# Moving one stage's weight preparation and statistics into the stage before it

## The chip, the cores and the metric

The kernel runs on one core of a Trainium2 chip. The metric is the device time of one execution in microseconds (us). Three timed runs of the kernel before gave 1868.03, 1863.23 and 1867.54 us; their median is 1867.54 us.

## The reference

Two decoder layers on x of 32 x 64 tokens of width 256 (2048 tokens in all). Every sub-layer normalises its input and adds its result to x. In order: layer 0 has a causal self-attention (16 heads of 128), a cross-attention to a context (16 heads of 8, no weights of its own), and a feed-forward block; layer 1 has a recurrent mixer, a cross-attention, and a feed-forward block with 4-bit weights. What matters here is the feed-forward block of layer 0:

```
n  = attention of 16 heads of 16 on rmsnorm(x, ln1_w)        # Wq, Wk, Wv, Wo
m  = modulation from n, through A (256 x 16) and B (16 x 1024)
h  = silu(z @ W_in.T + m @ B) * (z @ W_up.T)                 # z = rmsnorm(.., ln2_w), 1024 wide
x  = x + h @ W_down.T
```

W_in, W_up and W_down are 256 x 1024 matrices (1 MB each). The norm's weight ln2_w is folded into W_in and W_up by scaling their rows.

## The kernel before

All 2048 tokens stay in SBUF as 16 tiles of 128 rows (`core.x`). The kernel is five stages, one after the other; inside a stage each engine has its own instruction list, written by hand, and engines meet only through semaphores. A stage consists of blocks. At the end of a block all engines meet in a barrier. Between two stages there is one more such meeting, in which SyncE clears the semaphores (`run_stage`). `run_steps` orders an engine's list: at step s it issues, for each part with lag l, the work of unit s - l, parts in the order in which they are listed. So an instruction that waits holds up everything listed behind it on its engine.

**Full-precision products from two parts.** Matmuls of the feed-forward part take operands split into a high part (rounded to fp32r, a ScalarE copy) and a low part (the difference, a subtraction), and add three products.

**Stage 2, `stage_L0_cross`.** First `token_stats` turns the statistics of each row (`bn_stats`, one per tile, L216) into mean and 1/std (L219 to L233). If the flag `core.stats_ready` is set, the 16 `bn_stats` are left out, because the stage before has gathered them; before the change this is so on entering stage 2 and not on entering stage 3. Then the main block runs 32 units (a tile has two: its two column halves). Per unit: TensorE makes scores (L801), VectorE takes the maximum and subtracts it (L721, L725), ScalarE exponentiates (L747), TensorE transposes in two halves (L813), ScalarE copies each half to SBUF (L753), TensorE weighs the values (L829), VectorE divides (L732, L735), GpSimd adds to x (L712). Once per tile GpSimd normalises x (L685) and builds the key operand (L689) and the value operand (L701), TensorE transposes x (L789), and ScalarE copies that out (L764). SyncE loads the context, four chunks of 768 KB.

ScalarE's list in a step s is: exponent of unit s-4, second half's copy of s-5, the x copy of s-2 (in every second step), first half's copy of s-4.

**Stage 3, `stage_L0_ffn`.** (a) `token_stats`, in whose block SyncE issues all weight loads of the stage (L1533, L1535, L1536: eight matrices, B three times, the norm weights ln); (b) `split_tokens`, which normalises, transposes and splits the 16 tiles (L280, L305, L296, L274); (c) a preparation block: it waits for all loads, scales and splits the attention's weights, scales W_in and W_up on VectorE (L1596) and computes part of the modulation (L1560, L1582); (d) `attention16`, 16 tiles. There ScalarE also makes the high parts of the three matrices and of B, one piece in each second step (L1613, L1619), and GpSimd, once it has done its own 16 tiles (L982, L985), clears two buffers (L1624) and makes the low parts (L1627, L1632); (e) `feed_forward`, which uses all parts. L1111 projects the values of one tile, L959 multiplies a small piece of the modulation (16 x 128) by its tanh.

Of the kernel before, what the change touches and what calls it, by code (L numbers as in the profile page):

```python
# [7 lines left out]
STAGES = "12345"  # L8

ALU = mybir.AluOpType  # L10
# [6 lines left out]
P = 128  # L17
# [595 lines left out]
def stage_L0_cross(core):  # L613
# [7 lines left out]
    with ExitStack() as octx:  # L621
# [22 lines left out]
        with ExitStack() as ctx:  # L644
# [26 lines left out]
            @block.sync  # L671
            def _(sp):
                load_context(sp, 1, NT // CHUNK)

            @block.gpsimd
            def _(pool):
# [38 lines left out]
                run_steps(pool, U, [(add, 5), (operands, 0), (values, 3)], unroll=2, head=U + 5)  # L715

            @block.vector
            def _(dve):
# [21 lines left out]
                run_steps(dve, U, [(shift, 3), (attended, 5)], unroll=2, head=U + 5)  # L740

            @block.scalar
            def _(act):
# [23 lines left out]
                run_steps(act, U, [(exponent, 4), (probT_copy(1), 5), (xT_copy, 2), (probT_copy(0), 4)], unroll=2,  # L767
# [81 lines left out]
def attention16(core, mode, tag, mv, rstd, factor, w, zT=None, mT=None, beside=None, prefetch=None):  # L849
# [6 lines left out]
    with ExitStack() as ctx:  # L856
# [116 lines left out]
        def _(pool):  # L973
# [33 lines left out]
            if beside:  # L1007
                beside[1](pool)

        @block.scalar  # L1010
        def _(act):
# [53 lines left out]
            def weights(i, rnd, k):  # L1065
                if i % 2 == 1 and i // 2 < len(beside[0]):
                    beside[0][i // 2](act)

            if not own:
                act.wait_ge(masks, 3)  # L1070
            if own:
                steps(act, [(probT_copy(0), 3), (tanh, 5), (operands, 0), (probT_copy(1), 3), (attT_copy, 4),
                            (exponent, 2), (weights, 0)])
# [419 lines left out]
def stage_L0_ffn(core):  # L1493
    nc, ins = core.nc, core.ins
    F, R = 1024, 16
    with ExitStack() as ctx:
# [10 lines left out]
        parts = {n: room.sb(n + "_parts", [P, 2, 2 * F], F32R) for n in ("in", "up", "down")}  # L1507


        w["B"] = room.sb("B", [64 + R, F])  # L1510
        b_high = room.sb("b_high", [64 + R, F], F32R)
        b_rows = room.sb("b_rows", [64 + R, F], F32R)
        m_rows = room.sb("m_rows", [64 + R, NT, P], F32R)
        w["all"] = room.sb("all", [P, 3, NC * F])
        for n, (name, c) in enumerate((("in", NC), ("up", NC), ("down", F // P))):
            w[name] = w["all"][:, n, :].rearrange("p (c n) -> p c n", c=c)
        high_done, low_done, zeroed = room.sems("high_done", "low_done", "zeroed")
        ln = room.sb("ln", [P, 2, NC])
        with ExitStack() as sctx:
            sroom = Room(nc, sctx, "s3w")  # L1520
            for n in ("wq", "wk", "wo"):
# [6 lines left out]
            loads = (("wq", "WqT"), ("wk", "WkT"), ("wv", "WvT"), ("wo", "L0_ffn_Wo"), ("A", "L0_ffn_A"),  # L1528
                     ("in", "WinT"), ("up", "WupT"), ("down", "WdownT"))

            def load_weights(sp):
                for dst, src in loads:
                    sp.dma_start(w[dst][:, :, :], ins[src].rearrange("(c p) n -> p c n", p=P)).then_inc(w_in, 16)  # L1533
                for at in (0, 32, 64):
                    sp.dma_start(w["B"][at:at + R, :], ins["L0_ffn_B"]).then_inc(w_in, 16)  # L1535
                sp.dma_start(ln[:, :, :], ins["ln_ffn"].rearrange("a (c p) -> p a c", p=P),  # L1536
                             allow_slow_non_contiguous=True).then_inc(w_in, 16)
# [6 lines left out]
            ALL = 16 * (len(loads) + 4)  # L1544
# [41 lines left out]
            def _(dve):  # L1586
# [6 lines left out]
                for names, norm in ((("wv",), 0), (("in", "up"), 1)):  # L1593
                    for n in names:
                        for c in range(NC):
                            nc.vector.tensor_scalar(w[n][:, c, :], w[n][:, c, :], ln[:, norm, c:c + 1], None, ALU.mult)  # L1596
                    if norm == 0:
                        dve.wait_ge(a2_high, 1)
                        nc.vector.tensor_tensor(a2_parts[:, 1, :, :], a2[:, :, :], a2_parts[:, 0, :, :], ALU.subtract) \
                            .then_inc(a2_low, 1)  # L1600
                for n, (raw, dst) in enumerate((("wq", "q_parts"), ("wk", "k_parts"))):
                    for c in range(NC):
# [3 lines left out]
                                                       op0=ALU.mult, op1=ALU.subtract)  # L1606
                dve.wait_ge(wa_full, 1)
# [3 lines left out]
        def high_part(name):  # L1611
            def part(act):
                nc.scalar.activation(parts[name][:, 0, :], flat(name), ACT.Copy).then_inc(high_done, 1)  # L1613
            return part

        def high_rows(act):
            act.wait_ge(zeroed, 2)
            for at, dst in ((0, b_rows), (32, b_rows), (64, b_high)):
                last = nc.scalar.activation(dst[at:at + R, :], w["B"][at:at + R, :], ACT.Copy)  # L1619
            last.then_inc(high_done, 1)  # L1620

        def low_parts(pool):
            for rows in (b_rows, m_rows):
                nc.gpsimd.memset(rows[:].bitcast(F32), 0.0).then_inc(zeroed, 1)  # L1624
            for n, name in enumerate(parts):
                pool.wait_ge(high_done, n + 1)
                nc.gpsimd.tensor_tensor(parts[name][:, 1, :], flat(name), parts[name][:, 0, :], ALU.subtract) \  # L1627
                    .then_inc(low_done, 1)
            pool.wait_ge(high_done, len(parts) + 1)
            pool.wait_ge(low_done, len(parts))  # L1630
            pool.wait_ge(zeroed, 2)
            nc.gpsimd.tensor_tensor(b_rows[64:64 + R, :], w["B"][64:64 + R, :], b_high[64:64 + R, :], ALU.subtract) \  # L1632
                .then_inc(low_done, 1)
            pool.wait_ge(low_done, len(parts) + 1)

# [796 lines left out]
```

## Time and profile before

| | |
|---|---|
| median of the timed runs | 1867.54 us |
| the profiled execution's own time | 1862.36 us |
| its span, first to last instruction | 1860.6 us |
| TensorE busy | 1647.9 us (89%) |
| VectorE busy | 1129.8 us (61%) |
| ScalarE busy | 843.3 us (45%) |
| GpSimd busy | 684.4 us (37%) |
| stage 2, entry to last instruction | 568.0 to 695.5 us |
| stage 3 begins; its attention block begins | 696.15; 731.55 us |

The page has one line for each engine with its busy time and share of the span. A high share of TensorE says that it is usually the bound, but a share over the whole span hides single places. These are to be seen in the timeline, which lists instructions in order of time, and in a table of windows.

### The profile page before, as it was taken

What the parts mean: (1) busy time and instruction counts of PE and PEld (TensorE: products, weight loads), DVE (VectorE), ACT (ScalarE), POOL (GpSimd) and SP (SyncE); (2) the same over time, 40 slices, a digit from 0 to 9 for tenths busy, and PEclk for the clock granted to TensorE, in tenths of its full rate; (3) what the DMA queues carried; (4) which work ended last, traced back from release to release, by engine and by line L of the source; (5) the groups of instructions that cost most, each with busy time, mean ns of one, the idle gap of its engine ahead of it and who ended that gap; (6) DMA issues with size and microseconds to landing.
All of it is one profiled execution on the core that took longest, in us unless ns stands there. A gap on an engine that the chain in (4) does not pass through costs nothing. (4 is left out here: it accounts for less than half of the span.)

```text
span 1860.6 us, 33694 instructions
## 1 busy us (share of the span) xinstructions
PE 1647.9 (89%) x12998; PEld 1277.9 (69%) x12998; DVE 1129.8 (61%) x1820; ACT 843.3 (45%) x1401; POOL 684.4 (37%) x508
## 2 busy tenths in 40 slices
PE   4999999999987886799999777999998598999997
PEld 3888888888874664687888542444445475888886
DVE  6667776777786875654432767999996475111111
ACT  3545555554544663444422336555552475322222
POOL 0121212111124642700432107999996340333332
PEclk9999999999998996899999778999999797999999
DMA  3011111111102002000120100000000910000001
GB/s 98 15 60 58 60 34 53 65 40 59 56 34 86 2 4 94 2 2 2 38 93 7 38 1 0 1 1 0 1 1 0 333 46 1 1 1 1 1 0 45
DMA packets 50354, 66.73 MB, mean 36 GB/s; under 512 B 7312, under 2 KB 43664, under 8 KB 49600
## 3 DMA queue, kind: packets, MB, share of 16 engines
q1 hardware_dynamic: 50240, 65.14, 10.4%
q8 instruction: 80, 1.31, 0.3%
q14 instruction: 34, 0.28, 0.1%
HBM read 45.86 MB, written 19.27 MB: 35 GB/s over the span
## 5 line engine op out<-in xcount | busy, mean ns | idle before, releaser
L546 POOL TENSOR_TENSOR s_w_parts<-s_w_raw,s_w_parts 128x768 fp32r<-128x768 f32 x16 | 29.6, 1851 | 429.2 <-ACT s_w_parts L498 429.2
L1327 DVE TENSOR_TENSOR s6f_hid<-s6f_act_sb,s6f_u_ps 128x512 f32<-128x512 f32 x64 | 44.0, 688 | 218.3 <-PE s6f_u_ps L1278 218.3
L1350 POOL TENSOR_TENSOR s6f_hid_parts<-s6f_hid,s6f_hid_parts 128x512 fp32r<-128x512 f32 x64 | 82.6, 1291 | 226.3 <-ACT s6f_hid_parts L1316 226.3
L1994 POOL TENSOR_TENSOR s4b_pcs<-s4b_cs,s_p_rows 128x1024 f32<-128x1024 f32 x64 | 120.6, 1908 | 95.3 <-ACT s4b_cs L2040 95.3
L2005 POOL TENSOR_TENSOR s4b_with_re<-s4b_with_re,s4b_with_im 128x1024 f32<-128x1024 f32 x64 | 150.6, 2378 | 2.6 <-DVE s4b_with_im L1959 2.6
L2080 PE MATMUL s4b_c_ps<-s4b_pcs,const 128*128 128x512 f32 x256 | 123.3, 605 | 0.0
L422 PE MATMUL s_v_ps<-s_wv_parts,s_xnT 128*128 128x256 f32 x768 | 104.5, 286 | 11.9 <-ACT s_v L527 6.3
L481 PE MATMUL s_o_ps<-s_w_parts,s_zT 128*128 128x256 f32 x768 | 109.3, 292 | 4.1 <-DVE x_rows L585 4.0
L422 PEld LDWEIGHTS s_v_ps<-s_wv_parts,s_xnT 128*128 128x128 f32 x768 | 96.9, 191 | 17.5 <-ACT s_v L527 9.6
L1316 ACT ACTIVATE s6f_hid_parts<-s6f_hid 128x512 fp32r<-128x512 f32 x64 | 40.5, 632 | 144.5 <-PE s6f_o_ps L1298 141.1
L2070 PE MATMUL s4b_turns_ps<-s_theta_bd,s_zc 128*128 128x512 f32 x128 | 77.6, 690 | 31.5 <-DVE s4b_frac L1944 30.4
L1350 POOL TENSOR_TENSOR s3f_hid_parts<-s3f_hid,s3f_hid_parts 128x512 fp32r<-128x512 f32 x32 | 42.3, 1321 | 171.0 <-ACT s3f_hid_parts L1316 171.0
L1298 PEld LDWEIGHTS s6f_o_ps<-s6w_parts,s6f_hid_parts 128*128 128x128 f32 x768 | 99.2, 188 | 6.7 <-issue 1.0
L1278 PE MATMUL s6f_g_ps<-s_zT,s6w_parts 128*128 128x512 f32 (+1 forms) x384 | 101.2, 398 | 1.2 <-PEq L260 1.2
L481 PEld LDWEIGHTS s_o_ps<-s_w_parts,s_zT 128*128 128x128 f32 x768 | 96.1, 191 | 8.9 <-issue 4.6
L440 PE MATMUL s_q_ps<-s_xnT,s_w_parts 128*128 128x512 f32 x384 | 102.1, 401 | 0.0
L1298 PE MATMUL s6f_o_ps<-s6w_parts,s6f_hid_parts 128*128 128x256 f32 x768 | 100.7, 280 | 0.8 <-POOL s6f_hid_parts L1350 0.8
L1278 PE MATMUL s6f_u_ps<-s_zT,s6w_parts 128*128 128x512 f32 (+1 forms) x384 | 100.4, 396 | 0.0
L440 PE MATMUL s_k_ps<-s_xnT,s_w_parts 128*128 128x512 f32 x384 | 98.5, 392 | 0.0
L511 ACT ACTIVATE s_ex<-s_sc 128x256 f32<-128x256 f32 x64 | 26.7, 417 | 144.3 <-DVE s_sc L579 144.3
L2080 PEld LDWEIGHTS s4b_c_ps<-s4b_pcs,const 128*128 128x128 f32 x256 | 49.4, 194 | 60.8 <-issue 58.5
L1278 PEld LDWEIGHTS s6f_u_ps<-s_zT,s6w_parts 128*128 128x128 f32 x384 | 72.3, 188 | 17.8
(308 smaller groups left out, 4028.5 us busy)
## 6 DMA issues: line engine op xcount, KB each, us to landing
stored_weights<-s1q_halves SPq DMA_DIRECT2D x16, 768.0 KB, 3.5
s6w_parts<-stored_weights SPq DMA_DIRECT2D x32, 384.0 KB, 7.9
s1q_packed<-in_codes SPq DMA_DIRECT2D x8, 384.0 KB, 4.4
s1q_scale<-in_scale_rows SPq DMA_DIRECT2D x8, 384.0 KB, 5.0
early_values<-s_vbd SPq DMA_DIRECT2D x1, 2176.0 KB, 12.0
s_vbd<-early_values SPq DMA_DIRECT2D x1, 2176.0 KB, 12.7
x_rows<-in_x SPq DMA_DIRECT2D x1, 2048.0 KB, 8.2
s_w_raw<-in_L_attn_W_Q SPq DMA_DIRECT2D x16, 128.0 KB, 2.2
```

The source lines that it names most:

```text
L422: last = nc.tensor.matmul(v_ps[:, n * 2 * E:(n + 1) * 2 * E], xnT[:, px, c, g * TG + t, :], wv_parts[:, pw, c, :, :], start=(c == 0 and (p ...
L440: last = nc.tensor.matmul(ps[:, :], weights(slot, pw, m, c), xnT[:, px, c, g * TG:(g + 1) * TG, :], start=(c == 0 and (pw, px) == PARTS[0] ...
L481: last = nc.tensor.matmul(o_ps[:, t // 2, (t % 2) * D:(t % 2 + 1) * D], zT[:, pz, t * P:(t + 1) * P], w_parts[:, k // G, pw, 2, :], start= ...
L1278: last = nc.tensor.matmul(ps[:, s, :], wt(pw, c, f), zT[:, pz, c:c + 1, bass.ds(rnd * TG, TG), :] .rearrange("p c t q -> p (c t) q"), star ...
L1298: last = nc.tensor.matmul(o_ps[:, t, 0:D], hid_parts[:, f % 2, ph, t * P:(t + 1) * P], down_w(pw, f), start=(f == 0 and (ph, pw) == PARTS[0]),
L1316: nc.scalar.activation(hid_parts[:, f % 2, 0, :], hid[:, f % 2, :], ACT.Copy).then_inc(high_done, 1)
L1327: nc.vector.tensor_tensor(hid[:, f % 2, :], act_sb[:, f % 2, :], u_ps[:, f % 2, :], ALU.mult) \
L1350: nc.gpsimd.tensor_tensor(hid_parts[:, f % 2, 1, :], hid[:, f % 2, :], hid_parts[:, f % 2, 0, :], ALU.subtract).then_inc(low_done, 1)
L1994: last = nc.gpsimd.tensor_tensor(pcs[:, half, n_, :].rearrange("p (k c) -> p k c", k=HK), cs[:, half, n_, :].rearrange("p (k c) -> p k c", ...
L2005: nc.gpsimd.tensor_tensor(with_re[:, half, n_, :], with_re[:, half, n_, :], with_im[:, half, n_, :], op).then_inc(sum_done, 1)
L2070: nc.tensor.matmul(turns_ps[:, :], zc[:, half, bass.ds(i * P, P)], theta_bd[:, half, n_ * 64:(n_ + 1) * 64, :].rearrange("p c m -> p (c m) ...
L2080: last = nc.tensor.matmul(c_ps[:, n_, b * 512:(b + 1) * 512], core.c("tri"), pcs[:, half, n_, b * 512:(b + 1) * 512], start=True, stop=True)
```

## The change

The two stages become one function with a common set of tiles and semaphores. The loads of W_in, W_up, W_down, B and ln move from stage 3's start to SyncE's list in stage 2's main block, behind the context. The scaling moves from VectorE (stage 3, block c) to ScalarE (stage 2, in place). The high parts stay on ScalarE and the low parts on GpSimd, but in stage 2, in pieces: one ScalarE instruction at the end of each step 8 to 20, one GpSimd instruction at the end of each step 14 to 25. One small subtraction (B's low part) moves from GpSimd in block d to VectorE in block c. VectorE in stage 2 takes the statistics of each finished tile, two steps behind the last addition to it.

```diff
+class FfnWeights:
+    def load(self, sp):
+        for name, src in (("in", "WinT"), ("up", "WupT"), ("down", "WdownT")):
+            sp.dma_start(self.raw(name), ins[src].rearrange("(c p) n -> p c n", p=P)).then_inc(self.loaded, 16)
+        for at in (0, 32, 64):
+            sp.dma_start(self.B[at:at + self.R, :], ins["L0_ffn_B"]).then_inc(self.loaded, 16)
+        sp.dma_start(self.ln[:, :, :], ins["ln_ffn"].rearrange("a (c p) -> p a c", p=P), ...)
+
+    def scalar(self, u, rnd, n):
+        step = u - 8
+        if step in (0, 1, 2, 3):
+            act.wait_ge(self.loaded, 112)
+            rows = self.all[:, step // 2, (step % 2) * F:(step % 2 + 1) * F]
+            nc.scalar.activation(rows, rows, ACT.Identity, scale=self.ln[:, 1, step % 2:step % 2 + 1]) ...
+        elif step in (4, 5, 6, 7, 8, 9):
+            act.wait_ge(self.scaled, 4)
+            nc.scalar.activation(self.parts[name][:, 0, at:at + F], self.all[:, (step - 4) // 2, at:at + F], ACT.Copy)
+        elif step in (10, 11, 12):
+            act.wait_ge(self.zeroed, 1)
+            nc.scalar.activation(dst[at:at + R, :], self.B[at:at + R, :], ACT.Copy).then_inc(self.high_done, 1)
+
+    def gpsimd(self, u, rnd, n):
+        if u == 0:
+            nc.gpsimd.memset(self.b_rows[:].bitcast(F32), 0.0).then_inc(self.zeroed, 1)
+        step = u - 14
+        if step in range(12):
+            pool.wait_ge(self.high_done, step // 2 + 1)
+            nc.gpsimd.tensor_tensor(self.parts[name][:, 1, at:at + C], self.all[:, step // 4, at:at + C],
+                                    self.parts[name][:, 0, at:at + C], ALU.subtract)   # C = 512
...
 # stage 2, main block
                 load_context(sp, 1, NT // CHUNK)
+                beside.load(sp)
-                run_steps(pool, U, [(add, 5), (operands, 0), (values, 3)], unroll=2, head=U + 5)
+                run_steps(pool, U, [(add, 5), (operands, 0), (values, 3), (beside.gpsimd, 0)], unroll=2, head=U + 5)
-                run_steps(dve, U, [(shift, 3), (attended, 5)], unroll=2, head=U + 5)
+                def gather_stats(u, rnd, n):
+                    if u % 2:
+                        dve.wait_ge(added, u + 1)
+                        nc.vector.bn_stats(core.stats[:, u // 2, :], core.x[:, u // 2, :])
+                run_steps(dve, U, [(shift, 3), (attended, 5), (gather_stats, 7)], unroll=2, head=U + 7)
+                core.stats_ready = True
-                run_steps(act, U, [(exponent, 4), (probT_copy(1), 5), (xT_copy, 2), (probT_copy(0), 4)], unroll=2,
+                run_steps(act, U, [(exponent, 4), (probT_copy(1), 5), (xT_copy, 2), (probT_copy(0), 4),
+                                (beside.scalar, 0)], unroll=2,
...
 # stage 3
-            loads = (("wq", "WqT"), ("wk", "WkT"), ("wv", "WvT"), ("wo", "L0_ffn_Wo"), ("A", "L0_ffn_A"),
-                     ("in", "WinT"), ("up", "WupT"), ("down", "WdownT"))
+            loads = (("wq", "WqT"), ("wk", "WkT"), ("wv", "WvT"), ("wo", "L0_ffn_Wo"), ("A", "L0_ffn_A"))
...
-                for names, norm in ((("wv",), 0), (("in", "up"), 1)):
-                    ...  nc.vector.tensor_scalar(w[n][:, c, :], w[n][:, c, :], ln[:, norm, c:c + 1], None, ALU.mult)
+                for c in range(NC):
+                    nc.vector.tensor_scalar(w["wv"][:, c, :], w["wv"][:, c, :], ln[:, 0, c:c + 1], None, ALU.mult)
...
+                nc.vector.tensor_tensor(early.b_rows[64:64 + R, :], early.B[64:64 + R, :], early.b_high[64:64 + R, :],
+                                        ALU.subtract)
...
-        def low_parts(pool):
-            for rows in (b_rows, m_rows):
-                nc.gpsimd.memset(rows[:].bitcast(F32), 0.0).then_inc(zeroed, 1)
-            for n, name in enumerate(parts):
-                pool.wait_ge(high_done, n + 1)
-                nc.gpsimd.tensor_tensor(parts[name][:, 1, :], flat(name), parts[name][:, 0, :], ALU.subtract) \
-                    .then_inc(low_done, 1)
...
+        def zero_rows(pool):
+            nc.gpsimd.memset(m_rows[:].bitcast(F32), 0.0).then_inc(zeroed, 1)
...
+def stage_L0_cross_and_ffn(core):
+    with ExitStack() as ctx:
+        early = FfnWeights(core, Room(core.nc, ctx, "s3e"))
+        stage_L0_cross(core, early)
+        stage_L0_ffn(core, early)
```

## Rows read from the trace of the kernel before

**Rows 1.** Timeline, stage 3's entry: start us, duration us, engine, line, operation, [idle before, releaser]

```profile
695.07 0.45 POOL L712 TENSOR_TENSOR x_rows<-x_rows,s_att 128x128 f32<-128x128 f32 x1 [1.46 <-DVE s_att L735]
696.17 1.28 ACT L238 ACT_TABLE_LOAD   x1 [2.51 <-PEq L168]
696.20 5.33 DVE L216 BATCH_NORM_STATS2 x_stats<-x_rows 128x6 f32<-128x256 f32 x16 [1.22 <-PEq L168]
...
701.56 1.17 DVE L219 BATCH_NORM_AGGREGATE s_mv<-x_stats 128x2 f32<-128x6 f32 x16
...
704.43 0.17 DVE L233 TENSOR_TENSOR s_factor<-s3n_inv,s_rstd 128x16 f32<-128x16 f32 x1
706.71 0.43 SPq L1536 DMA_DIRECT2D s_ln<-in_ln_ffn  x1
707.59 1.06 DVE L280 TENSOR_SCALAR s3t_xn<-x_rows,s_mv,s_factor 128x256 f32<-128x256 f32 x3 [2.98 <-PEq L189]
```

**Rows 2.** Timeline, the same place on entering stage 2, where the statistics were ready

```profile
569.66 0.25 DVE L221 RECIPROCAL s_rstd<-s2n_std 128x16 f32<-128x16 f32 x1 [0.43 <-ACT s2n_std L238]
570.24 5.71 PE L779 MATMUL s_o_ps<-const 128*128 128x512 f32 x8 [5.56 <-PEq L189]
```

**Rows 3.** Timeline, stage 3's preparation block

```profile
722.10 2.73 DVE L1596 TENSOR_SCALAR s_all<-s_all,s_ln 128x1024 f32<-128x1024 f32 x4
722.23 8.45 PE L1560 MATMUL s3w_m_ps<-s_zT,s3w_a_parts 128*128 128x512 f32 x24 [0.64 <-DVE s3w_a_parts L1599]
```

**Rows 4.** Timeline, the attention block, GpSimd and VectorE

```profile
768.20 4.56 POOL L1627 TENSOR_TENSOR s_in_parts<-s_all,s_in_parts 128x2048 fp32r<-128x2048 f32 x1
768.70 13.12 DVE L959 SCALAR_TENSOR_TENSOR s_mT<-s_mT,s3a_th 16x128 f32<-16x128 f32 x1
...
777.19 4.49 POOL L1627 TENSOR_TENSOR s_down_parts<-s_all,s_down_parts 128x2048 fp32r<-128x2048 f32 x1
```

**Rows 5.** Windows, one per tile: PE, PEld, DVE, ACT, POOL busy; clock, DMA, GB/s

```profile
757.88:765.80 7.92, 7.92 (x127) 6.62 (x127) 4.45 (x7) 3.56 (x7) 7.59 (x9) 1.00 0.01 2
765.80:783.61 17.81, 8.46 (x127) 6.75 (x126) 17.18 (x8) 5.63 (x9) 15.88 (x5) 0.78 0.01 1
783.61:792.67 9.06, 9.06 (x127) 7.76 (x126) 4.07 (x8) 3.11 (x6) 0.00 (x0) 0.87 0.02 4
792.67:801.12 8.45, 8.00 (x128) 6.63 (x127) 4.26 (x8) 5.18 (x9) 0.00 (x0) 1.00 0.01 2
```

**Rows 6.** Timeline, one pair of steps in stage 2's main block

```profile
676.53 1.06 ACT L747 ACTIVATE s_ex<-s_sc 128x1024 f32<-128x1024 f32 x1
...
677.65 0.66 PE L813 MATMUL s_pT_ps<-const,s_ex 128*128 128x128 f32 x4 [0.16 <-ACT s_ex L747]
...
678.34 0.60 ACT L753 ACTIVATE s_probT<-s_pT_ps 128x512 f32<-128x512 f32 x1 [0.26 <-PE s_pT_ps L813]
...
679.53 1.06 ACT L747 ACTIVATE s_ex<-s_sc 128x1024 f32<-128x1024 f32 x1 [0.59 <-DVE s_sc L725]
679.64 0.69 PE L801 MATMUL s_s_ps<-s_kbd,s_xT 32*64 32x256 f32 x16 [0.17 <-DVE s_sc L725]
```

**Rows 7.** Windows: stage 2's first steps, a steady pair; stage 3's splitting of tokens

```profile
576.20:583.40 7.20, 4.59 (x46) 2.26 (x46) 4.90 (x4) 3.19 (x5) 5.68 (x5) 1.00 0.41 141
676.20:683.30 7.10, 6.33 (x114) 4.60 (x114) 5.78 (x9) 4.41 (x8) 4.54 (x5) 1.00 0.01 3
...
712.00:714.00 2.00, 2.00 (x7) 0.91 (x8) 2.00 (x7) 1.16 (x4) 0.00 (x0) 0.50 0.06 14
```

**Rows 8.** Single lines: shortest/median/longest duration in ns, first and last start

```profile
L1350 POOL TENSOR_TENSOR s3f_hid_parts<-s3f_hid,s3f_hid_parts x32: 1269/1288/1937, 889.2 to 1024.3; 128x512 fp32r<-128x512 f32 x32
L725 DVE TENSOR_TENSOR s_sc<-s_s_ps,s_mx x32: 1224/1224/1226, 578.7 to 688.8; 128x1024 f32<-128x1024 f32 x32
```

**Rows 9.** Timeline, stage 2: SyncE's last context load, ScalarE's exponent in step 9

```profile
574.01 0.51 SPq L636 DMA_DIRECT2D s_vrow<-in_ctx_values  x1
...
598.06 1.06 ACT L747 ACTIVATE s_ex<-s_sc 128x1024 f32<-128x1024 f32 x1
```

More of the change, by code:

```diff
@@ L6 @@
 from concourse import mybir
-STAGES = "12345"
+STAGES = "1245"
 ALU = mybir.AluOpType
@@ L614, in stage_L0_cross @@
+def stage_L0_cross(core, beside):
     nc, ins = core.nc, core.ins
@@ L1007, in _ @@
             if beside:
-                beside[1](pool)
+                beside(pool)
         @block.scalar
@@ L1072, in _ @@
                 steps(act, [(probT_copy(0), 3), (tanh, 5), (operands, 0), (probT_copy(1), 3), (attT_copy, 4),
-                            (exponent, 2), (weights, 0)])
+                            (exponent, 2)])
             else:
@@ L1506, in stage_L0_ffn @@
         w["WoA"] = room.sb("WoA", [P, NC, R])
[L1507 to L1512, printed above, removed]
+        parts, ln = early.parts, early.ln
+        w["all"] = early.all
+        for name in ("in", "up", "down"):
+            w[name] = early.raw(name)
         m_rows = room.sb("m_rows", [64 + R, NT, P], F32R)
[L1514 to L1518, printed above, removed]
+        (zeroed,) = room.sems("zeroed")
         with ExitStack() as sctx:
@@ L1543, in stage_L0_ffn @@
             block = sctx.enter_context(nc.Block())
-            ALL = 16 * (len(loads) + 4)
+            ALL = 16 * len(loads)
             @block.tensor
@@ L1592, in _ @@
                         .then_inc(a2_done, 1)
-                for names, norm in ((("wv",), 0), (("in", "up"), 1)):
[L1594 to L1600, printed above, removed]
+                for c in range(NC):
+                    nc.vector.tensor_scalar(w["wv"][:, c, :], w["wv"][:, c, :], ln[:, 0, c:c + 1], None, ALU.mult)
+                dve.wait_ge(a2_high, 1)
+                nc.vector.tensor_tensor(a2_parts[:, 1, :, :], a2[:, :, :], a2_parts[:, 0, :, :], ALU.subtract) \
+                    .then_inc(a2_low, 1)
                 for n, (raw, dst) in enumerate((("wq", "q_parts"), ("wk", "k_parts"))):
@@ L1636, in flat @@
-        def flat(name):
-            return w[name][:, :, :].rearrange("p c n -> p (c n)")
+        def zero_rows(pool):
+            nc.gpsimd.memset(m_rows[:].bitcast(F32), 0.0).then_inc(zeroed, 1)
         def part_of(name):
             return lambda part, c, f: parts[name][:, part, c * F + f * P:c * F + (f + 1) * P]
-        attention16(core, "ffn", "s3a", mv, rstd, factor, w, zT, mT, beside=([high_part(n) for n in parts] + [high_rows], low_parts))
+        attention16(core, "ffn", "s3a", mv, rstd, factor, w, zT, mT, beside=zero_rows)
@@ L1643, in stage_L0_ffn @@
         feed_forward(core, "s3f", zT, part_of("in"), part_of("up"),
-                     lambda part, f: parts["down"][:, part, f * D:(f + 1) * D], F, ACT.Silu, (mT, m_rows, b_rows),
+                     lambda part, f: parts["down"][:, part, f * D:(f + 1) * D], F, ACT.Silu, (mT, m_rows, early.b_rows),
                      stats=True, early=EarlyKeys(core, room, w))
         core.stats_ready = True
+def stage_L0_cross_and_ffn(core):
[3 more added lines that the diff above has]
+        stage_L0_ffn(core, early)
```

59 lines of the change are left out of this document (34 added, 25 removed).

## The prediction

> **What bounds the kernel now.** I read the page first: TensorE is busy for 89% of the span, so work taken from another engine is worth nothing unless TensorE was waiting for it. The places where it waits are then to be found, and the timeline around the edit shows two.
>
> The first is stage 3's entry [rows 1]. TensorE and GpSimd finish stage 2 at 695.52 and nothing is multiplied again before 708. In between VectorE takes 16 statistics (696.20, 5.33 us), aggregates them (until 702.73) and has the factor ready at 704.60. The next row of VectorE starts only at 707.59, after 2.98 us of idleness that a barrier ended: SyncE still issued loads until 707.14, and the barrier of the block waits for SyncE too. The same chain on entering stage 2, with ready statistics and two loads, ends at 569.91, and TensorE starts at 570.24 [rows 2]: a barrier with nobody late costs 0.33 us.
>
> The second is in the attention block [rows 4]. GpSimd starts its three subtractions of 128x2048 at 768.20; they end at 777.19 + 4.49 = 781.68. VectorE's 16x128 multiplication, L959, starts at 768.70 and ends at 781.82, after 13.12 us, and everything behind it on VectorE waits. The windows show what it does to the tile [rows 5]: 17.81 us from one projection to the next, where the tile of the same parity two later takes 8.45 us; the next takes 9.06 us against 7.92 us, with the clock at 0.87 because TensorE had stood still. So the stall costs 9.36 + 1.14 = 10.5 us.
>
> In stage 2 no engine is full [rows 7]: in a pair of steps of 7.1 us TensorE is busy for 6.33, VectorE for 5.78, GpSimd for 4.54, ScalarE for 4.41 us. It is bound by a loop through several engines, and ScalarE is part of it.
>
> **The change part by part.**
>
> *Statistics in stage 2.* The 5.33 us go from the entry. VectorE then aggregates from 696.20 to 697.37, but ScalarE's table load (696.17, 1.28 us) ends at 697.45; from there the tail of 704.60 - 702.73 = 1.87 us leads to 699.32. SyncE has then five loads instead of twelve; at the 0.43 us of the last one it is done by 698.4; so the barrier costs 0.33 us and the splitting starts at 699.65 in place of 707.59: -7.9 us, of which 5.3 are the statistics and 2.6 SyncE's queue [rows 1, 2]. In stage 2 sixteen statistics of 0.33 us, one in each second step, join 5.78 busy us of 7.1 [rows 7]; VectorE idles 1.3 us per pair, so fifteen are hidden. The last one can start only when GpSimd's last addition has landed: +0.4 us at the stage's end. Its wait is for an addition two steps old; nothing queues behind it for long.
>
> *One meeting fewer between the stages.* 695.52 to 696.17 is 0.65 us [rows 1] against 0.33 us for a plain barrier [rows 2]: -0.3 us. Bounds 0 and -0.65.
>
> *Scaling leaves VectorE in the preparation block.* Four instructions, 2.73 us [rows 3]. They lie beside TensorE's 24 matmuls, which run from 722.23 to 730.68 and end the block. The added subtraction of B's low part is shorter than what goes. Worth 0.
>
> *The low parts leave the attention block.* GpSimd's three 4.5 us instructions go, and with them the stall: -10.5 us. L959 then meets GpSimd with one buffer to clear at most, before it starts. ScalarE's high parts go too; the windows without and with such a piece (757.88, 792.67 [rows 5]) are 7.92 and 8.45 us, the normal times of their parity, so that is worth 0. The Trainium skill's page "SBUF — State Buffer", section "Who interferes with whom", says that a VectorE instruction with two SBUF inputs and a GpSimd instruction that reads SBUF exclude each other for a whole instruction. By that rule L959 would have waited for one subtraction, some 4 us, and the gain would be some 9 us smaller. The trace disagrees in the amount: it waited for all three.
>
> *ScalarE in stage 2.* Thirteen instructions of 1024 columns. The nearest row is the exponent of 128x1024, 1.06 us [rows 6]; back to back they overlap slightly, so I take 1.0 us each. By busy time they fit (4.41 + 2.1 of 7.1 us), but not by order. In an even step the new one stands between the first half's copy and the exponent of 676.53, which starts without any idle time and for which TensorE waits 0.16 us at 677.65. It delays that by 1.0 us. TensorE's later scores (679.64) wait for VectorE instead and have about 0.25 us of slack: +0.75 us. In the odd step the copy of 678.34 comes 1.0 us late, the new instruction takes 1.0 us, and the exponent of 679.53 has 0.59 us of idle time before it and some 0.2 us of overlap to give: it is 1.2 us late, the transposition behind it 1.1 us. So a pair costs 1.1 us and a lone even step 0.75 us. Steps 8 to 20 are six pairs and one even step: 6.6 + 0.75 = +7.3 us. Bounds: 0, if the order adjusts and ScalarE's idle 2.7 us per pair take them up; 13 x 1.06 = 13.8 us, if every one lies on the loop. I take 7.3, which is what the rows give link by link.
>
> *GpSimd in stage 2.* Twelve subtractions of 128x512 at 1.29 us [rows 8]. A pair of steps holds 4.54 + 2.58 = 7.12 us, exactly its length, and longer than that in no step in which ScalarE also stretches it. What waits for GpSimd (keys, values, the next x) is due two to three steps later. Cost 0; bound 12 x 1.29 = 15.5 us, were GpSimd already the bound. VectorE's instructions here read PSUM with at most one SBUF operand; L725 takes 1224 to 1226 ns in all 32 cases [rows 8], although GpSimd's key operand runs beside some of them: no stall of L959's kind. The cleared buffer at step 0 stands behind the first operands, for which TensorE waits: 0.
>
> *Loads in stage 2.* SyncE reaches them at 574.5 [rows 9]. In stage 3 more than the same bytes were issued from 696.2 on and traffic had died down by 712 (0.06 share [rows 7]), 16 us later; so they land by 590.5. ScalarE needs them behind step 8's copy, just before the exponent at 598.06 [rows 9]: 7.6 us to spare. Cost 0; without that cover the wait would hold the whole loop, one for one.
>
> *Clock.* TensorE starts again at 700 in place of 708, having stood still for 5.6 us in place of 13.7. In stage 2 the clock was 0.5 after a pause of such a length (5.56 us idle [rows 2]), so I expect 1.2 GHz in both cases and the same 8.45 us for the matmuls.
>
> **Sum.** -7.9 - 0.3 - 10.5 + 7.3 + 0.4 = -11.0 us. The profiled execution took 1862.36 us (span 1860.6): 1851.4 us by that. It was the fastest of four known executions, whose mean is 1865.3 us; the forecast is set against that mean: 1854.3, so 1854 us.
>
> **Rivals.**
>
> *Hidden in stage 2.* Only the 0.4 us remain: -18.3 us, 1847 us. For it: ScalarE's 2.7 us idle per pair. Against: exponent and transposition stand end to end at 676.53.
>
> *Stage 2 pays in full.* 13.8 us from ScalarE, or GpSimd at its limit: -4.5 us, 1861 us. For it: GpSimd's 7.12 us of 7.1.
>
> *The stall does not go.* L959 in tile 0 is its first use, and the cause might be its own: then -0.5 us, 1865 us. Against: it ends 0.14 us after GpSimd's last subtraction, and starts 0.5 us after the first [rows 4].
>
> *Slower: the clock falls in stage 2.* The stretched pairs (8.2 us for 6.33 busy, 77%) might take TensorE from 2.4 to 1.2 GHz in the middle of the stage. Against it: the first steps have 4.59 busy of 7.2 us (64%) and keep 1.00 [rows 7]; for it: in the splitting of the tokens the clock stays at 0.50 with TensorE shown as fully busy [rows 7]. The price: the tile at a mean clock of 0.87 spent 26% of its time at 0.5 and took 1.14 us more [rows 5]; all of it at 0.5 would have added 4.4 us to 7.92, a factor of 1.55. A slow pair of steps is then 6.33 x 1.55 = 9.8 us, 2.7 more than 7.1. The rest of the change gives 18.3 us, so it turns slower from the seventh such pair on; over the 13 pairs after step 10 it gives 35 - 18.3 = +17 us, 1882 us. The Trainium skill ("TensorE: Matmul & The Clock Gate", "What's actually happening") says that throttled is the default state and activity releases it; that is the rule by which this rival would come about.
>
> **How the numbers follow.** Forecast 0.58, hidden 0.13, paid in full 0.16, the stall stays 0.06, slow clock 0.07. The range runs from 1843 (hidden, set against the fastest execution) to 1865 (paid in full, set against the slowest); the clock and most of the stall case are left out. A measurement of this kernel tells 0.3%, 5.6 us, from no change. Faster by more: the forecast, the hidden case and part of the full price, 0.77. Within: the rest of that and the stall, 0.15. Slower: 0.08.
>
> **What would show it.** Right: VectorE's splitting starts about 4 us after stage 3's table load; no L959 above 1 us; tiles of 7.9 and 8.4 us throughout; stage 2 about 7.7 us longer, with pairs of 8.2 us from step 8 to 20 and of 7.1 us before and after, ScalarE never waiting for a DMA. Wrong: a ScalarE wait for the loads at step 8, pairs that stay long after step 20 (GpSimd), a granted clock below 1 in stage 2, or a long VectorE instruction beside one of GpSimd's.

## The result and the profile after

The changed kernel takes 1901.73 us (median of four runs, 1900.59 to 1904.27). The kernel before, timed beside it, takes 1865.38 us (1861.46 to 1868.03). The ratio is 1.0197, with a 95% interval of 1.0181 to 1.0213: 36 us slower, where 11 us faster was forecast.

The head of the page after, with engines and clock:

```profile
span 1898.8 us, 33691 instructions
...
PE 1705.3 (90%) x12998; PEld 1317.2 (69%) x12998; DVE 1117.6 (59%) x1817; ACT 848.0 (45%) x1408; POOL 683.4 (36%) x516
...
PEclk9999999999987555799999786999999798999999
```

TensorE has 57 busy us more than before (1647.9) for the same matmuls, while the other engines moved by some 12 us at most. So its matmuls became slower. The last row says where: each digit is a fortieth of the span, 47.5 us, and the three fives cover 617 to 760 us, most of stage 2. Windows of the after kernel place the fall exactly (us, busy PE, PEld, DVE, ACT, POOL, clock, DMA share, GB/s):

```profile
598.00:599.00 1.00, 0.53 (x11) 0.29 (x17) 0.97 (x4) 0.64 (x2) 0.08 (x1) 1.00 0.00 0
600.00:601.00 1.00, 0.07 (x3) 0.00 (x0) 0.82 (x1) 1.00 (x2) 1.00 (x2) 1.00 0.00 0
602.00:603.00 1.00, 1.00 (x19) 0.97 (x18) 0.96 (x3) 1.00 (x2) 0.44 (x1) 0.76 0.00 0
603.00:604.00 1.00, 1.00 (x19) 0.42 (x17) 0.13 (x1) 1.00 (x2) 0.79 (x2) 0.50 0.00 0
690.00:701.24 11.24, 10.77 (x114) 7.70 (x114) 6.33 (x9) 4.52 (x8) 6.99 (x8) 0.50 0.01 2
```

The last of them is one pair of steps, to be set beside the pair in [rows 7]: the same 114 matmuls take 10.77 busy us in place of 6.33 at clock 0.50, which is 1.2 GHz, in place of 1.00, 2.4 GHz. The pair is 11.24 us long in place of 7.13. The timeline of the after kernel around 600 us shows what came just before, and further on what else answers to the prediction:

```profile
581.12 0.69 PE L874 MATMUL s_s_ps<-s_kbd,s_xT 32*64 32x256 f32 x16 [1.68 <-DVE s_sc L791]
...
599.12 1.15 ACT L653 ACTIVATE s3e_all<-s3e_all,s3e_ln 128x1024 f32<-128x1024 f32 x1
600.16 1.05 ACT L819 ACTIVATE s_ex<-s_sc 128x1024 f32<-128x1024 f32 x1
601.26 0.66 PE L886 MATMUL s_pT_ps<-const,s_ex 128*128 128x128 f32 x4 [1.20 <-ACT s_ex L819]
602.43 1.06 PE L886 MATMUL s_pT_ps<-const,s_ex 128*128 128x128 f32 x4
602.45 1.14 ACT L653 ACTIVATE s3e_all<-s3e_all,s3e_ln 128x1024 f32<-128x1024 f32 x1
...
634.96 1.27 POOL L675 TENSOR_TENSOR s3e_in_parts<-s3e_all,s3e_in_parts 128x512 fp32r<-128x512 f32 x1
...
678.73 0.38 ACT L836 ACTIVATE s_xT<-s_x_ps 128x256 f32<-128x256 f32 x1 [4.96 <-PE s_x_ps L862]
689.97 0.38 ACT L836 ACTIVATE s_xT<-s_x_ps 128x256 f32<-128x256 f32 x1 [4.96 <-PE s_x_ps L862]
...
752.30 0.45 POOL L778 TENSOR_TENSOR x_rows<-x_rows,s_att 128x128 f32<-128x128 f32 x1 [2.43 <-DVE s_att L801]
752.78 0.43 DVE L809 BATCH_NORM_STATS2 x_stats<-x_rows 128x6 f32<-128x256 f32 x1 [0.23 <-POOL x_rows L778]
753.48 1.28 ACT L238 ACT_TABLE_LOAD   x1 [3.09 <-PEq L709]
753.52 1.17 DVE L219 BATCH_NORM_AGGREGATE s_mv<-x_stats 128x2 f32<-128x6 f32 x16 [0.30 <-PEq L709]
...
756.45 0.17 DVE L233 TENSOR_TENSOR s_factor<-s3n_inv,s_rstd 128x16 f32<-128x16 f32 x1
756.95 1.06 DVE L280 TENSOR_SCALAR s3t_xn<-x_rows,s_mv,s_factor 128x256 f32<-128x256 f32 x3 [0.33 <-PEq L189]
```

At 599.12 ScalarE runs its first new instruction, a scaling, and the exponent behind it is late. TensorE stands still for 1.20 us, and between 602 and 603 the clock falls. It stays at 0.50 for the rest of stage 2. GpSimd's first subtraction comes 32 us later and has no part in that. (VectorE's first statistic starts at 598.8, just before; the run with the statistics alone, below, clears it.) The first of the rows shown speaks against a simple rule: at 581.12 the same stage has a pause of 1.68 us, longer than this one, and the clock was still 1.00 at 598. In front of it stand spare matmuls of 512 columns. The length of a pause alone can therefore not be what decides.

Set stage by stage against the profile before, in us:

| | before | after | difference |
|---|---|---|---|
| start of stage 2's main block | 570.24 | 571.49 | +1.25 |
| main block to the end of the last addition or statistic | 125.3 | 181.7 | +56.4 |
| from there to the table load | 0.65 | 0.27 | -0.4 |
| table load to the first splitting | 11.42 | 3.47 | -7.95 |
| splitting and preparation, up to the first value projection | 27.2 | 27.1 | -0.1 |
| first to last value projection (L1111; L1180 after) | 133.5 | 122.7 | -10.8 |
| the rest | 992.3 | 992.1 | -0.2 |

These add up to the +38.2 us by which the span grew. Everything outside stage 2 went as forecast; all that was gained, and twice as much again, went in one row. The attention block in windows of its own, first before, then after (columns as above):

```profile
734.81:868.30 133.49, 117.69 (x1829) 98.93 (x1828) 74.55 (x97) 58.98 (x96) 48.00 (x37) 0.95 0.01 2
```

```profile
784.04:906.70 122.66, 115.75 (x1827) 97.38 (x1828) 61.23 (x97) 50.69 (x90) 31.04 (x32) 0.99 0.01 2
```

In this block VectorE has 13.3 busy us less, of which 12.8 are the one long L959 of [rows 4]. Its counterpart after, from the view of one line (shortest, median, longest in ns; first and last start):

```profile
L1032 DVE SCALAR_TENSOR_TENSOR s_mT<-s_mT,s3a_th x16: 272/279/280, 817.7 to 921.7; 16x128 f32<-16x128 f32 x16
```

### The profile page after: what moved, and what is told of

It reads as the page before. It is cut to its first block and busy times, and to the rows that moved or that the text cites. A ratio compares the mean times of both kernels' runs of the same rounds, so it can differ in the third digit from the quotient of the medians.

```text
span 1898.8 us, 33691 instructions
## 1 busy us (share of the span) xinstructions
PE 1705.3 (90%) x12998; PEld 1317.2 (69%) x12998; DVE 1117.6 (59%) x1817; ACT 848.0 (45%) x1408; POOL 683.4 (36%) x516
```

## The experiments

The theory was now: ScalarE's pieces cost little by themselves, but the pause that the first makes for TensorE lets the clock fall, and the stage at 1.2 GHz does not come back. The rivals: the pieces are dear in themselves, by ScalarE's order or GpSimd's load; or the loads of 3 MB that now run in stage 2 disturb it. Each time stands beside the kernel before on the same chip: 1866.32 us (median of 10 runs) in one set, 1865.13 us (median of 18) in the other.

**One piece alone, in the kernel before.** No loads, no weights, no statistics: a single useless ScalarE copy of 128x1024.

```diff
+                def one_piece(u, rnd, n):
+                    if u == 8:
+                        nc.scalar.activation(spare[:, 1, :], spare[:, 0, :], ACT.Copy)
-                run_steps(act, U, [..., (probT_copy(0), 4)], ...
+                run_steps(act, U, [..., (probT_copy(0), 4), (one_piece, 0)], ...
```

> The kernel before with a single additional ScalarE copy of 128x1024 (from one spare tile to another, of no use) at the end of step 8. Theory C: one pause of about 1.2 us is enough; the clock falls to 0.50 near 602 us and stays there for the 13 pairs left, each 4.1 us longer (11.24 against 7.13 us): + 53 us, 1918 us. If the pause only topples it in some executions, the runs are split between 1865 and 1918. Rival L: one piece costs 0.75 us, as reckoned before: 1866 us.

Measured: 1920.18 us (1917.80 to 1923.14) against 1866.32; ratio 1.0299, 1.0275 to 1.0323. Timeline and windows of this run:

```profile
599.04 1.06 ACT L775 ACTIVATE s_spare<-s_spare 128x1024 f32<-128x1024 f32 x1
601.10 0.66 PE L824 MATMUL s_pT_ps<-const,s_ex 128*128 128x128 f32 x4 [1.11 <-ACT s_ex L753]
```

```profile
602.00:604.00 2.00, 2.00 (x32) 1.23 (x28) 0.92 (x3) 1.94 (x3) 1.33 (x3) 0.59 0.00 0
610.00:690.00 80.00, 76.69 (x830) 54.77 (x814) 42.62 (x57) 32.85 (x51) 33.11 (x36) 0.50 0.01 1
```

One instruction of 1.06 us costs 54 us. It makes a pause of 1.11 us, and 1 to 2 us later the clock is down, to the end of the stage (the 1.68 us pause near its start stands in this trace too, at 1.00); the x copies that follow are 11.25 us apart. Neither the loads nor GpSimd nor the number of pieces is needed for it.

**Half of that piece.** The same with 128x512.

```diff
-                        nc.scalar.activation(spare[:, 1, :], spare[:, 0, :], ACT.Copy)
+                        nc.scalar.activation(spare[:, 1, 0:512], spare[:, 0, 0:512], ACT.Copy)
```

> As the run with one useless ScalarE copy at step 8 (1920 us), the copy half as long: 128x512, 0.6 us, so that TensorE's pause there is about 0.65 us in place of 1.11 us. If the fall depends on the length of the pause, the clock stays at 1.00 and the kernel takes 1866 us (+ 0.3 us). If any lengthening topples it, 1918 us; if it is at the edge, some runs show the one and some the other.

Measured: 1867.16 us (1863.98 to 1870.87, ten runs) against 1865.13; ratio 1.0005, 0.9995 to 1.0015. Timeline and window of this run:

```profile
600.04 0.63 ACT L775 ACTIVATE s_spare<-s_spare 128x512 f32<-128x512 f32 x1
601.67 0.66 PE L824 MATMUL s_pT_ps<-const,s_ex 128*128 128x128 f32 x4 [0.68 <-ACT s_ex L753]
```

```profile
606.00:680.00 74.00, 65.26 (x1179) 47.16 (x1178) 59.99 (x84) 46.42 (x74) 46.95 (x52) 1.00 0.01 2
```

A pause of 0.68 us in the same place leaves the clock at 1.00. One pair is 7.41 us long, all others 7.13. So an extra instruction in this place is not enough: the two runs differ only in the copy's length, and with it in TensorE's pause. That holds for this step of this loop and is no rule for pauses at large, as the 1.68 us pause behind the spare matmuls shows. Between 0.68 and 1.11 us nothing was tried.

**The change with the pause filled.** In PE's steps 9 to 21, two spare matmuls of 256 columns, issued just before the one that waits for the exponent.

```diff
+                def hold_clock(u, rnd, n):
+                    if 9 <= u <= 21:
+                        for _ in range(2):
+                            nc.tensor.matmul(x_ps[:, D:2 * D], core.c("ident"), core.c("age")[:, 0:D],
+                                             start=True, stop=True)
-                run_steps(pe, U, [..., (weigh(0), 5), (turn(0), 4), ...
+                run_steps(pe, U, [..., (weigh(0), 5), (hold_clock, 0), (turn(0), 4), ...
```

> The changed kernel with two spare matmuls of 128x256 ahead of each first transposition in TensorE's steps 9 to 21, where it waits for the delayed exponent; nothing else is moved. Theory C: TensorE is never still for long, the clock stays at 1.00, and my blind sum holds: pairs of 8.2 us from step 8 to 20, then 7.1 us; 1851 us by the profile's own time, up to 7 us more where the filler (26 x 0.28 us) is not hidden: 1851 to 1860 us. Rival L: more work on TensorE in a stage that is too full makes it slower, above 1900 us.

Measured: 1856.88 us (1856.39 to 1860.53, seven runs) against 1866.32; ratio 0.9960, 0.9946 to 0.9975. Timeline and window of this run:

```profile
600.05 1.13 PE L858 MATMUL s_x_ps<-const 128*128 128x256 f32 x4
```

```profile
612.38 1.04 ACT L819 ACTIVATE s_ex<-s_sc 128x1024 f32<-128x1024 f32 x1
613.10 1.13 PE L858 MATMUL s_x_ps<-const 128*128 128x256 f32 x4
614.07 0.60 PE L892 MATMUL s_pT_ps<-const,s_ex 128*128 128x128 f32 x4
```

```profile
598.00:650.00 52.00, 48.70 (x730) 35.34 (x728) 38.15 (x55) 37.89 (x54) 34.64 (x36) 1.00 0.01 2
```

With every piece in its place and useless work added to TensorE, the kernel is 45 us faster than the changed one, and the clock never leaves 1.00. Seven pairs are long, 8.84 us twice, 8.74 us four times and 8.1 us once, together 10.8 us over 7 x 7.13. (The profile counts each spare matmul as two records.) That holds ScalarE's pieces and the spare matmuls, which no run parts; the forecast had 7.3 us for the pieces alone. The trace hints at the share: in an odd step the exponent is over at 613.42, but the transposition starts at 614.07, behind the spare matmuls. Without these 0.65 us a pair of 8.74 us would be 8.1 us long, an estimate, where 8.2 was forecast.

**The change with ScalarE's pieces where ScalarE is idle.** Before each x copy ScalarE waits 1.84 us. The pieces go there, one in each even step from 8 to 30 and the last in step 31; GpSimd's start four steps later, because the high parts are later.

```diff
-        step = u - 8
+        step = (u - 8) // 2 if u % 2 == 0 and u >= 8 else 12 if u == 31 else None
...
-        step = u - 14
+        step = u - 18
...
-                run_steps(act, U, [(exponent, 4), (probT_copy(1), 5), (xT_copy, 2), (probT_copy(0), 4),
-                                (beside.scalar, 0)], unroll=2,
+                run_steps(act, U, [(exponent, 4), (probT_copy(1), 5), (beside.scalar, 0), (xT_copy, 2),
+                                (probT_copy(0), 4)], unroll=2,
```

> The changed kernel with ScalarE's thirteen pieces in another place of its list: in even steps between the second half's copy and the x copy, where it idles for 1.84 us, every second step from 8 on (the last in step 31); GpSimd's pieces start at step 18. Theory C (clock): what the change costs is TensorE's clock, which fell to 0.50 at 602.4 us, after one pause of 1.2 us behind the first piece, and does not come back by itself; in the gap no piece makes TensorE wait, so the clock stays at 1.00, a pair of steps stays at 7.1 us, the stage at 125 to 128 us, and the kernel takes 1844 us (1862.4 - 18.3), a few us more if GpSimd is at its limit. Rival L (load): the added work itself is too much for the stage, wherever it stands; then it stays near 1900 us. Between: 1850 to 1890 would mean that the clock falls later, by GpSimd.

Measured: 1849.91 us (1849.35 to 1851.24) against 1866.32; ratio 0.9919, 0.9896 to 0.9941. Timeline and windows of this run:

```profile
645.84 1.05 ACT L658 ACTIVATE s3e_up_parts<-s3e_all 128x1024 fp32r<-128x1024 f32 x1
647.78 0.38 ACT L836 ACTIVATE s_xT<-s_x_ps 128x256 f32<-128x256 f32 x1 [0.90 <-PE s_x_ps L862]
```

```profile
598.00:640.00 42.00, 37.33 (x680) 27.14 (x681) 36.06 (x54) 32.47 (x48) 28.69 (x32) 1.00 0.01 2
640.00:697.00 57.00, 48.31 (x874) 35.33 (x872) 46.30 (x73) 40.45 (x60) 43.30 (x47) 1.00 0.01 2
```

The x copy still has 0.90 us of idle time before it with the piece in place, the pairs are 7.13 or 7.14 us long but for the last (7.35, with pieces in two steps in a row), and stage 3's table load comes at 697.01 against 696.17 before. This version does all the work of the change and is as fast as any that was run: 52 us faster than the changed kernel and 16 us faster than the one before. The thirteen pieces cost almost nothing there. Two things were changed at once, the place in the list (two places earlier) and the spacing (one piece in two steps). At step 8, where both versions have their first piece, the place alone differs, and with it TensorE's wait for the next exponent: 1.20 us in the changed kernel, 0.16 us here. What the spacing adds was not tested.

**No spare matmuls at the stage's start, in the kernel before.** Stage 2's first steps hold matmuls of 512 columns whose result is not used (`keep_busy`); here they are left out.

```diff
-                run_steps(pe, U, [(keep_busy(4, 0), 2), (scores, 3), (keep_busy(1, 1), 3), (weigh(0), 5), ...
+                run_steps(pe, U, [(scores, 3), (weigh(0), 5), ...
```

> The kernel before without the spare matmuls at the start of stage 2 (4 x 128x512 and two more): does the stage's own work raise the clock? Theory C in its strong form: no; the stage runs from its first pair to its last at 0.50, 16 pairs at 11.24 in place of 7.13 us, less some 5 us of spare matmuls: + 60 us, 1925 us. Rival: the stage warms itself within a few us, as its TensorE is busy for 6.33 of 7.13 us: 1860 to 1870 us.

Measured: 1926.18, 1925.88, 1869.98 and 1928.29 us. Their mean clocks are 0.904, 0.904, 0.944 and 0.903, so they are two outcomes of one kernel, and a median says nothing. Window of the first of them:

```profile
600.00:750.00 150.00, 143.85 (x1532) 102.83 (x1530) 79.62 (x108) 60.59 (x94) 56.98 (x65) 0.50 0.01 2
```

Where the stage was not brought up to 2.4 GHz at its start, it ran at 1.2 GHz to its end in this profile, with pairs of 11.25 us, and two more runs have the same time. In the fourth run, of which there is no profile, the time and the mean clock say that it came up. So the loop does not always stay at the low clock.

**The changed kernel with a burst in step 24.** Twelve spare matmuls of 256 columns, once, after the pieces are done.

```diff
+                def warm_again(u, rnd, n):
+                    if u == 24:
+                        for _ in range(12):
+                            nc.tensor.matmul(x_ps[:, D:2 * D], core.c("ident"), core.c("age")[:, 0:D],
+                                             start=True, stop=True)
```

> The changed kernel with one dense burst of twelve spare 128x256 matmuls in TensorE's step 24 of stage 2, when ScalarE's pieces are over and the clock is at 0.50. If stage 2 can live at either clock and only keeps the one it has (theory C), the burst (about 6 us) brings it to 1.00, and it stays: the last five or six pairs take 7.1 in place of 11.2 us, 1901.7 + 6 - 23 = 1885 us. Rival: something else since the change holds the clock down (GpSimd's pieces, the statistics), so it falls again at once: 1901.7 + 6 = 1908 us.

Measured: 1889.35 us (1887.18 to 1889.65) against 1865.13; ratio 1.0123, 1.0105 to 1.0141. Timeline and windows of this run:

```profile
685.77 7.67 PE L858 MATMUL s_x_ps<-const 128*128 128x256 f32 x24
```

```profile
602.00:690.00 88.00, 82.92 (x844) 59.08 (x844) 47.19 (x67) 43.92 (x63) 45.13 (x47) 0.50 0.01 1
690.00:735.00 45.00, 39.96 (x677) 29.91 (x678) 32.16 (x50) 25.56 (x40) 23.03 (x27) 1.00 0.01 2
```

During the burst the clock comes back, and the same loop that did not raise it for 88 us then holds it: the x copies are 7.13 us apart from 695.29 on. The burst costs 7.67 us and the kernel is 12 us faster for it than the changed one.

**The statistics alone, in the kernel before.** Only VectorE's part of the change.

```diff
+                def gather_stats(u, rnd, n):
+                    if u % 2:
+                        dve.wait_ge(added, u + 1)
+                        nc.vector.bn_stats(core.stats[:, u // 2, :], core.x[:, u // 2, :])
-                run_steps(dve, U, [(shift, 3), (attended, 5)], unroll=2, head=U + 5)
+                run_steps(dve, U, [(shift, 3), (attended, 5), (gather_stats, 7)], unroll=2, head=U + 7)
+                core.stats_ready = True
```

> The kernel before with the statistics alone moved into stage 2; loads, scaling and splitting as before. It parts the 7.9 us of the entry. Theory S (SyncE sets the entry): VectorE's chain ends at 699, but the barrier still waits for SyncE, which issues loads until 707.1; the splitting of the tokens starts as late as before, + 0.4 us for the last statistic: 1866 us, the same as before. Rival: the statistics alone are worth their 5.3 us: 1861 us. And the clock in stage 2 stays at 1.00, as the statistics never make TensorE wait; if it falls, they share in the loss.

Measured: 1865.80 us (1862.78 to 1870.85, ten runs) against 1865.13; ratio 1.0004, 0.9993 to 1.0016. Timeline of this run:

```profile
701.41 0.18 DVE L233 TENSOR_TENSOR s_factor<-s3n_inv,s_rstd 128x16 f32<-128x16 f32 x1
702.71 6.63 SPq L1541 DMA_DIRECT2D s_B<-in_L_ffn_B  x3
709.38 0.42 SPq L1542 DMA_DIRECT2D s_ln<-in_ln_ffn  x1
```

The factor is ready at 701.59, but SyncE issues loads until 709.80, and the block's barrier waits for it. The 5.33 us of statistics are gone and nothing is won; the three small loads of B alone hold SyncE for 6.63 us. So the statistics are worth nothing as long as SyncE's loads stand there. The loads alone were not moved; by the rows of the kernel before VectorE's chain would then have ended at 704.60, for a gain of some 2.7 us, an estimate. The 7.95 us need both parts of the change. In stage 2 of this run every steady pair is 7.13 or 7.14 us long and the clock is 1.00, so VectorE's statistics have no part in the fall. In the changed kernel the same three issues take 7.32 us of SyncE in stage 2, where no barrier is near.

**The good version with one spare matmul per tile in stage 3's splitting**, to raise the clock before the preparation block.

```diff
-            split_tokens(core, zT, mv, factor, "s3t")
+            split_tokens(core, zT, mv, factor, "s3t", warm=1)
...
+                for _ in range(warm):
+                    nc.tensor.matmul(spare_ps[:, 0:D], core.c("ident"), core.c("age")[:, 0:D],
+                                     start=True, stop=True)
```

> The version with ScalarE's pieces in the gap (1849.9 us), and one spare matmul of 128x256 after each tile in the splitting of the tokens of stage 3, to a PSUM bank of its own, so that the preparation block's 24 matmuls (8.1 us at mostly 0.50) and the first attention tile run at 1.00. Theory C: -1.6 us for the matmuls and -1.4 us for the first projection, +1 us while the splitting is still at the low clock: 1848 us. Rival: the spare matmuls delay the transpositions for all 16 tiles (about 0.2 us each): 1851 to 1853 us.

Measured: 1850.59 us (1848.11 to 1852.42) against 1865.13; ratio 0.9920, 0.9902 to 0.9938. Windows of this run, then of the version without:

```profile
698.00:712.00 14.00, 10.93 (x58) 9.13 (x59) 11.13 (x40) 6.38 (x17) 0.00 (x0) 0.77 0.26 77
724.00:735.00 11.00, 7.09 (x104) 6.31 (x106) 2.82 (x5) 2.44 (x4) 9.78 (x11) 1.00 0.01 2
```

```profile
698.00:712.00 14.00, 10.08 (x32) 4.86 (x32) 11.78 (x41) 7.06 (x19) 0.00 (x0) 0.51 0.27 77
724.00:735.00 11.00, 8.55 (x102) 7.68 (x104) 2.16 (x5) 1.86 (x3) 10.52 (x12) 0.84 0.01 2
```

The clock rises as intended, from 0.51 to 0.77 and from 0.84 to 1.00, but the time is that of the version without, whose ratio of 0.9919 is the same within the intervals. The expected gain is a miss, and the rows between the two windows show where it went. First this run, then the version without:

```profile
716.62 7.33 PE L1622 MATMUL s3w_m_ps<-s_zT,s3w_a_parts 128*128 128x512 f32 x24 [1.47 <-DVE s3w_a_parts L1658]
718.00:720.00 2.00, 2.00 (x7) 1.56 (x6) 1.55 (x3) 0.59 (x1) 0.00 (x0) 0.52 0.00 0
726.46 1.69 PE L1168 MATMUL s3a_qk_ps<-s_zT,s_q_parts 128*128 128x256 f32 x12 [2.51 <-DVE s3a_mask_r L994]
726.00:728.00 2.00, 1.54 (x12) 1.49 (x12) 0.40 (x2) 0.00 (x0) 1.85 (x4) 1.00 0.06 12
```

```profile
715.13 7.37 PE L1618 MATMUL s3w_m_ps<-s_zT,s3w_a_parts 128*128 128x512 f32 x24 [0.64 <-DVE s3w_a_parts L1654]
725.00 2.52 PE L1164 MATMUL s3a_qk_ps<-s_zT,s_q_parts 128*128 128x256 f32 x12 [2.51 <-DVE s3a_mask_r L990]
725.00:727.00 2.00, 2.00 (x11) 2.00 (x12) 0.00 (x0) 0.00 (x0) 1.92 (x3) 0.63 0.00 0
```

The preparation's 24 matmuls start 1.5 us later, because the splitting with its spare matmuls ends later, and they are no shorter (7.33 us against 7.37): TensorE pauses for 1.47 us in front of them, and from 718 on the clock is down again, to 0.52. Only the attention block's first matmuls gain, and that gives the 1.5 us back. The rival with the delayed transpositions came true in part. The rows show one thing more: in front of the attention block TensorE pauses for 2.51 us in both versions, and behind it the clock is 0.63 in the one and 1.00 in the other. Again a pause of one length goes with both outcomes.

## Why the prediction was wrong

The step that failed is the clock in stage 2. The forecast took it to stay at 1.00, with pairs of 8.2 us; it fell to 0.50 at the first piece, the pairs took 11.24 to 11.8 us, and the stage grew by 56.4 us where 7.7 were forecast. Of the clock the prediction worked out only stage 3. The case that came about stood among the rivals, as "the clock falls in stage 2", with 0.07, and it too was wrong in three points.

- **Its evidence against.** The first steps, 64% busy at 1.00 [rows 7], were taken to show that the stage can be sparser and stay warm. But those steps hold the spare matmuls. Left out, three runs of four are as slow as a stage at 0.50, and the profiled one shows it; the fourth is not. What kept the clock there was left unread in the same window: 46 matmuls for 4.59 busy us, 100 ns each, where the steady pair has 56 ns (6.33 / 114). The rows that bore on the case were of another kind of work. They also held a pause of 1.68 us at 1.00, longer than the one that later did the harm, so the length of the pause read by itself would have spoken for the forecast as well.
- **What makes it fall.** I argued with the busy share of a stretched pair, 77%. No stretched pair was needed: it fell at the first piece, behind a single pause. The run with that one copy shows that this is enough, the one with the pause filled that without it the clock stays. That pause was forecast: an existing wait of 0.16 us plus 1.0 us, and it measured 1.20. The number was there and I asked only what it costs in time. Why this pause fells the clock, and the 1.68 us pause twenty us earlier does not, stays open; what TensorE did before each differs.
- **Its price.** 2.7 us per slow pair was forecast, 4.1 measured (11.24 - 7.13). The factor 1.55 is a slip in the working: the 26% are a share of the slow tile's 9.06 us, 2.36 us, in which only 2.36 - 1.14 = 1.22 us worth of work was done. That is a factor of 1.93, and 5.9 us more per pair (6.33 x 0.93). The tile also held other matmuls than the pair. The pair's own busy time grew by 1.70 (10.77 / 6.33), and with TensorE shown as busy for 96% of the pair nothing else could take it up. The pair grew by 4.1 and not by the 4.4 of busy time, because its idle time shrank from 0.8 to 0.5 us. With 4.1 in place of 2.7 the rival's own sum over its 13 pairs would have been 53 - 18.3 = +35 us, and the measured difference is 36. That the two agree so closely is in part luck: the sum leaves out what the pieces still cost at 1.2 GHz, about 2 us, and the 1.25 us in front of the stage.

The Trainium skill says that throttled is the default state and that activity releases the clock ("TensorE: Matmul & The Clock Gate", "What's actually happening"). The runs agree: without spare matmuls the profiled stage is at 0.50 throughout, and a burst of them releases the clock. What this rule alone does not tell is that the steady loop, with TensorE shown as busy for 96% of the time, does not release it.

The other steps, by the runs:

- **Entry of stage 3:** -7.9 forecast, -7.95 measured; that the statistics bring something only together with SyncE's part is shown by the run with the statistics alone. The forecast's shares, 5.3 for the statistics and 2.6 for SyncE's queue, are not shown: the statistics alone gained nothing. One meeting fewer: -0.3 against -0.4. Last statistic: +0.4, as it came.
- **The stall in the attention block:** -10.5 against -10.8, and no multiplication of that line above 0.28 us. The Trainium skill's rule of exclusion for one instruction ("SBUF — State Buffer", "Who interferes with whom") would have made the gain some 9 us smaller; the measured gain does not bear that amount out. That the two engines exclude each other at all fits both profiles, and no run parted it from other causes.
- **Scaling leaves the preparation block:** worth 0 forecast; -0.1 us for splitting and preparation together.
- **GpSimd and the loads:** 0 forecast. With the pieces in the gap and the clock at 1.00, twelve GpSimd pieces and all loads left the pairs at 7.13 us (the last at 7.35). ScalarE's first piece started without a wait for a DMA.
- **ScalarE's pieces:** +7.3 forecast in the place they were given, between 0 and 10.8 by the run with the filled pause; at 1.2 GHz, where ScalarE has time, only about 0.3 us in most pairs (11.55 against 11.24). The cover that the rival "hidden" named, 2.7 idle us per pair, exists, but the change does not put the pieces there. Put there, the kernel gives 1849.9 us, near that rival's 1847.
- **The range:** its ends follow only roughly from the words given for them. Hidden against the fastest execution gives 1862.4 - 18.3 = 1844, paid in full against the slowest 1868.0 - 4.5 = 1863.5. Nothing hangs on it.

The first +1.25 us in the table lie before any changed instruction, and after the attention block the good version's profile gives back 4.4 us of the 17.2 that it had gained (851.1 against 868.3 at the last value projection, 1847.8 against 1860.6 at the end). Of these, 2.3 us lie in the rest of stage 3, where the granted clock is 0.98 in place of 1.00 over equal stretches of 158.9 us, and 2.2 us in stage 4. Runs of the kernel before alone lie 7 us apart, and what moves these few us was not found.

## What to carry to other kernels

Before putting work beside a stage in which TensorE runs small matmuls with short gaps, ask for each piece how long it makes TensorE stand still once, not only what it adds to the loop, and price the stage at the other clock. These runs give no length below which a pause is safe; look at the granted clock of the new trace. Put the piece where its engine is idle anyway, in front of an instruction that waits for something else: here the place in the list, with the spacing that it brought, decided between 16 us gained and 36 us lost. And where a barrier ends a block, look at SyncE's issues too, because work removed in front of it may have been waiting with them.

## What the runs showed that was not expected

- In the profiles the loop of stage 2 keeps whichever clock it has until something disturbs it: pairs of 7.13 us at 1.00 or of 11.24 us at 0.50, over 125 and 150 us, with the same instructions. At 0.50 TensorE is shown as busy for 96% of the time and the clock still does not rise; 7.67 us of 256-column matmuls raised it.
- One pause of 1.11 us (a useless copy of 1.06 us) cost 54 us, and one of 0.68 us in the same step nothing. In the same traces a pause of 1.68 us behind spare matmuls of 512 columns left the clock at 1.00, and in front of the attention block one of 2.51 us went with 1.00 in one version and with a fall in another. What the work before a pause has to do with it was not tested on its own.
- Without the spare matmuls at its start the same kernel has two times, about 1926 and 1870 us. What decides between them in a run was not found.
- Three DMA issues of the small matrix B hold SyncE's queue for 6.2 to 7.6 us in these traces (6.23 in the kernel before, 7.57 in the version with the pieces in the gap), where one of a 1 MB matrix takes 0.5 to 0.8 us.
